# Half 0's new cell ahead of half 1's sum on VectorE, and half 0's cell tanh ahead of half 1's gate tanh on ScalarE, in a four-layer residual stack

## The reference, cut to what matters

```python
def step(carry, xw_t):
    prev_h, prev_c = carry
    A = xw_t + prev_h @ Wh
    i = jax.nn.sigmoid(A[:, 0:Hdim])
    f = jax.nn.sigmoid(A[:, Hdim:2 * Hdim])
    o = jax.nn.sigmoid(A[:, 2 * Hdim:3 * Hdim])
    g = jnp.tanh(A[:, 3 * Hdim:4 * Hdim])
    next_c = f * prev_c + i * g
    next_h = o * jnp.tanh(next_c)
    return ((next_h, next_c), next_h)
```

## Time and profile before

| | |
|---|---|
| median of 3 runs | 3879.23 us (3876.97 to 3882.91) |
| the profiled execution | 3882.09 us |
| its span, first to last instruction | 3880.3 us |
| TensorE matmul / VectorE / ScalarE / GpSimd busy | 3606.7 / 3369.5 / 1632.7 / 784.1 us |
| chain that ended last | VectorE 69%, TensorE 21%, issue 5%, ScalarE 4% |

### The profile page before, as it was taken

One profiled execution on the slowest core, in us unless ns is written; L12 is line 12 of the kernel. 1 busy time (PEld: TensorE's weight loads), 2 busy tenths in 40 slices (PEclk: granted clock), 3 DMA queues, 4 the chain that ended last, 5 costly groups with the idle time before them and its releaser, 6 DMA issues.

```text
span 3880.3 us, 256505 instructions
## 1 busy us (share of the span) xinstructions
PE 3606.7 (93%) x110398; PEld 3050.5 (79%) x110398; DVE 3369.5 (87%) x21169; ACT 1632.7 (42%) x8276; POOL 784.1 (20%) x3623
## 2 busy tenths in 40 slices
PE   7899999999999999999999999999999999999875
PEld 4688888888888888888888888888888888887754
DVE  6598888888898889888888898888888888888876
ACT  4244444444444444444444444444444444444332
POOL 1122222222222222222222222222222222222111
PEclk9999999999999999999999999999999999999999
DMA  7100000000000000000000000000000000000000
GB/s 278 49 7 7 10 10 10 7 7 10 10 10 10 8 7 9 10 10 10 10 7 7 10 10 10 10 7 7 10 10 10 10 9 7 9 7 7 7 6 8
DMA packets 19126, 63.41 MB, mean 16 GB/s; under 512 B 3958, under 2 KB 4526, under 8 KB 14914
## 3 DMA queue, kind: packets, MB, share of 16 engines
q1 hardware_dynamic: 17692, 46.67, 3.8%
q10 hardware_dynamic: 294, 0.33, 0.0%
HBM read 38.48 MB, written 8.39 MB: 12 GB/s over the span
## 4 chain that ended last, share of the span: by engine, by line
DVE 69%; PE 21%; issue 5%; ACT 4%; DMA 1%; POOL 0%; SPq 0%; ACTq 0%; DVEq 0%; POOLq 0%
DVE lstm_sums L743 20%; PE ps_lstm L1045 18%; DVE ps_lstm L748 9%; DVE lstm_ig_fc L754 6%; DVE rnn_sums L851 6%; DVE ps_lstm L759 4%; DVE lstm_h_parts L783 4%; DVE rnn_h_parts L861 3%; DVE lstm_h_scaled L780 3%; DVE rnn_h_parts L866 2%; DVE ps_rnn L759 2%; DVE lstm_h_parts L787 2%; DVE lstm_gates_2c L763 2%; DVE ps_rnn L856 2%; ACT rnn_h L506 2%
## 5 line engine op out<-in xcount | busy, mean ns | idle before, releaser
L1045 PE MATMUL ps_lstm<-lstm_Wh_parts,lstm_h_parts 128*20 128x256 f16 x65472 | 1971.5, 273 | 230.1 <-DVE lstm_h_parts L787 154.9
L1045 PEld LDWEIGHTS ps_lstm<-lstm_Wh_parts,lstm_h_parts 128*20 128x20 f16 x65472 | 1564.5, 91 | 612.2 <-DVE lstm_h_parts L787 486.4
L483 ACT ACTIVATE lstm_gates_2c<-ps_lstm 128x32 f32<-128x32 f32 x2048 | 405.0, 198 | 1416.4 <-DVE ps_lstm L748 1416.4
L743 DVE STREAM_TRANSPOSE lstm_sums<-ps_lstm 128x256 f32<-128x256 f32 x2048 | 912.6, 446 | 84.2 <-PE ps_lstm L1045 44.6
L347 POOL COPY lstm_sums<-lstm_in 128x32 f32<-128x32 f32 x2048 | 427.7, 211 | 1749.7 <-DVE ps_lstm L748 1749.7
L1084 PE MATMUL ps_rnn<-rnn_Wh_parts,rnn_h_parts 128*20 128x128 f16 x32736 | 640.8, 220 | 26.1 <-DVE rnn_h_parts L866 22.1
L1084 PEld LDWEIGHTS ps_rnn<-rnn_Wh_parts,rnn_h_parts 128*20 128x20 f16 x32736 | 546.6, 92 | 67.9 <-DVE rnn_h_parts L866 47.4
L748 DVE TENSOR_REDUCE ps_lstm<-lstm_sums 128x32 f32<-128x96 f32 x2048 | 554.5, 271 | 34.2
L488 ACT ACTIVATE lstm_o_scaled<-lstm_gates_2c 128x8 f32<-128x8 f32 x2048 | 426.9, 208 | 32.3
L783 DVE TENSOR_TENSOR lstm_h_parts<-lstm_o_scaled,lstm_tanh_c 128x8 f16<-128x8 f32 x2048 | 332.4, 162 | 108.4
L506 ACT ACTIVATE rnn_h<-ps_rnn 128x16 f32<-128x16 f32 x1024 | 188.6, 184 | 521.3 <-DVE ps_rnn L856 521.3
(11 more groups left out here) (189 smaller groups left out, 3140.0 us busy)
## 6 DMA issues: line engine op xcount, KB each, us to landing
layer_plus_2I<-in_L_cond_w SPq DMA_DIRECT2D x16, 1024.0 KB, 6.4
out<-out_rows SPq DMA_DIRECT2D x128, 64.0 KB, 1.7
x_rows<-in_x SPq DMA_DIRECT2D x31, 256.0 KB
lstm_Wx<-in_L_cond_Wh SPq DMA_DIRECT2D x1, 4096.0 KB, 17.9
lstm_Wx<-in_L_cond_Wx SPq DMA_DIRECT2D x1, 4096.0 KB, 13.6
layer_plus_2I<-in_L_cond_Wh SPq DMA_DIRECT2D x1, 1024.0 KB, 8.7
rnn_Wx<-in_L_cond_Wx SPq DMA_DIRECT2D x1, 1024.0 KB, 11.0
lstm_in<-in_L_cond_w SPq DMA_DIRECT2D x1, 1024.0 KB, 9.9
```

Source lines behind the costliest of these rows:

```text
L743: return mark(V.transpose(tr[h][s % 2][:, :, 0:QC], psL[h][:, 0:HW].rearrange("p (g c) -> p g c", c=QC)))
L1045: ins = mm(psL[h][QC * j:QC * j + LO + NB, 0:HW], hls[:, k, :], whl[:, k, h, e, j, :], start=(k == 0 and e == 0), stop=(k == KB - 1 and e ...
```

## The change

Two calls change places, each with its neighbour. No instruction is added, removed or altered, and every wait stays with its call. On ScalarE the cell tanh of half 0 now stands in front of the gate tanh of half 1. On VectorE the new cell of half 0 stands in front of half 1's sum.

```diff
@@ -495,8 +495,8 @@
                     if w["lstm"]:
                         gates(0, s)
                         out_gate(0, s)
+                        tanh_cell(0, s)
                         gates(1, s)
-                        tanh_cell(0, s)
                         out_gate(1, s)
                         tanh_cell(1, s)
                     if s == 0 and p["rnn"]:
@@ -884,8 +884,8 @@
                         reduce(0, s, at)
                         at = transpose(1, s)
                         p_at = products(0, s)
+                        new_cell(0, p_at)
                         reduce(1, s, at)
-                        new_cell(0, p_at)
                         if w["rnn"]:
                             r_at = transpose_rnn(s)
                         p_at = products(1, s)
```

## The result

The changed kernel takes 4048.46 us (median of 5 runs, 4046.80 to 4049.59) against 3879.23 before: a ratio of 1.0434, 95% interval 1.0423 to 1.0445, that is 169 us slower. The forecast was 4045 in 4030 to 4066. The profiled execution took 4048.1 with a span of 4046.3, 166.0 more than the span before; the prediction had put it at 4048. Most of the 3.5 us between the forecast and the median are the 2.9 that the prediction took off because the profiled execution before lay above its median; the one after does not.

The account below looks back on a forecast made before the run. The prediction took a 3.58 us step loop through VectorE and TensorE as the bound, VectorE alone in some steps. 1024 × 0.165 = 169, less 2 to 4, gave +166: 4045 us by median, range 4030 to 4066.

Parts of the forecast that it names:

- The new cell waits for products 0: VectorE: half 0's new cell needs its products' result, so it starts 0.035 us after they end and VectorE idles.
- Its slot in front of the sum: VectorE: half 1's sum starts 0.075 us behind the new cell, at 2095.42 instead of 2095.25, 0.165 later.
- Sum 1, gate tanh 1, products 1 have no slack: Half 1's sum, gate tanh and products all come 0.165 us later, moving TensorE's start by the same.
- Nothing is gained by the early tanh: Half 0's h stands behind half 1's products, so its earlier cell tanh gains nothing; bounds 0.01 gained, 0.03 lost.
- Swallowed time: Steps where TensorE is late by itself absorb 0.03 us each, 2 to 4 us in all.
- The ScalarE swap costs nothing: ScalarE: half 0's cell tanh ends at 2095.715, just as half 1's gate tanh is ready, so nothing is lost.
- the sum that waits until the new cell has finished: Rival on VectorE: half 1's sum comes 0.29 us late in place of 0.165, giving 4173 us; 3 in 100.
- Products 1 hang on the gate tanh: Half 1's products follow its gate tanh by 0.03; the rival has the RNN's transpose hold them, 3976 us, 3 in 100.
- The rival in which TensorE's clock falls: Rival: TensorE's clock falls in the last 32 steps, at most 43 us on top, 4088 us; 2 in 100.

Follow-up runs that it names:

- The filler in that wait: Changed kernel with one more VectorE instruction, on constants and waiting for nothing, between half 0's products and its new cell: 4048.20 us.
- fillers: Kernel before with one or two added VectorE instructions, on constants and waiting for nothing, in front of half 1's sum: 3919.38 us with one, 3999.56 with two.
- the runs with the added matmuls: Three more matmuls a step on TensorE in the last chunk: 4046.05 us on the changed kernel, 4049.64 on the kernel with the VectorE swap alone.
- the order that uses the early tanh: Changed kernel with half 0's h and high part in front of half 1's products, and half 1's new cell last: 3975.88 us.

## Why the prediction was right

The mechanism and the number held, step by step.

- *The new cell waits for products 0.* Forecast 0.035 behind their end. In the step shown the cell starts at 2183.25, 0.03 behind 2183.06 + 0.16. The filler in that wait, which cost nothing, shows that VectorE idles there.
- *Its slot in front of the sum.* Forecast 0.075, measured 0.08 to 0.09 (2183.25 to 2183.34); in return the sum lasts 0.26 and not 0.27. The two nearly cancel: sum 1 starts 0.17 later and ends 0.165 later. The prediction had neither of these two small errors in view; that they cancel is luck, worth some 7 us.
- *Sum 1, gate tanh 1, products 1 have no slack.* Shown by fillers: 80 us for 0.077 more.
- *Nothing is gained by the early tanh.* The VectorE swap alone takes the same time as both. Half 0's h stands behind products 1, 0.10 as before.
- *Swallowed time.* Forecast 2 to 4 us. Added up over all steps, TensorE's start behind the low part of half 0 came 2.4 us closer. 1024 × 0.165 is 169, less 2.4 and plus the 1.6 of the clock in the last chunk is 168; the span grew by 166.0. The last 2 us are within what one execution differs from another, so the hit to the microsecond is luck, the one to the few is not.
- *The ScalarE swap costs nothing.* Right in the changed kernel, but only because the later sum hides it: alone it costs 140 us. The prediction found the cell tanh ending just as the gate tanh becomes ready, and did not say that this holds only beside the other edit.

Of the rivals, the sum that waits until the new cell has finished would have given 4173; it starts 0.09 behind the cell's start, while the cell lasts 0.17. The Trainium skill, page "VectorE: DVE Perf Modes", section "The DRAIN you can't avoid", has the next op wait for an empty pipe, and adds that an op that is not held, by a rule that it gives further on, starts earlier. The prediction quoted the first half only. The runs go against it for these instructions and with the second: starts are 0.08 to 0.09 apart at 0.17 each. Products 1 hang on the gate tanh (0.03 behind it) and not on the RNN's transpose. The rival in which TensorE's clock falls came true for 3.4 us of the last chunk, where I had written that the level should stay: I had compared the busy share of ordinary steps and not the steps of the last chunk, whose gaps grew from 1.65 and 1.83 us in the kernel before to 1.82 and 2.03. The price, 1.6 us, is far below the bound of 43. The page "TensorE: Matmul & The Clock Gate" of the Trainium skill, in its section "Why this matters for your kernels", warns of idle gaps between bursts; the runs with the added matmuls agree in direction, though the gaps here are shorter than the one it warns of.

The misses were in the experiments: the spacing behind a 16-element product, in front of an instruction without a wait, is 0.08 where I took 0.09 to 0.11 (41 us for one filler, not 65 to 85), the gate tanh follows a cell tanh after 0.08 where I took 0.09 to 0.17 (140, not 171 or more), and in the order that uses the early tanh VectorE's own queue, which sets the time of many steps, was left out (3976, not 3943).

## What to carry to other kernels

In an in-order queue an instruction moved forward takes its wait with it: ask when its operand is ready and who stands behind it, and not how early its own reader could start. Two halves that share a queue are a balance; before favouring one, look for the instruction of the other half that its reader also stands behind. And price two edits both together and each alone when they delay the same instruction: here 169 and 140 make 169, and either of them undone by itself would have left most of the loss.

## What the runs showed of the hardware that was not expected

- A gate tanh (128x32) starts 0.08 us behind the start of a cell tanh (128x8) that lasts 0.18, and then lasts 0.19 in place of 0.20; the cell tanh behind a gate tanh starts after 0.10.
- Half 1's sum lasts 0.26 instead of 0.27 right behind a small instruction that writes PSUM (a filler or the new cell), with the same shape and data. There it also no longer waits for its transpose; which of the two shortens it no run separates.
- TensorE's clock fell to the 1.2 GHz level in the middle of a chunk that had run at 2.4 GHz, behind idle gaps of 1.8 to 2.0 us a step; before the change, with gaps of 1.65 to 1.83 in the same chunk, it did not, nor with gaps of up to 1.98 behind two fillers. Three matmuls a step in the gaps kept it up in the two kernels with the fall that were given them; each of these is one execution. Whether a given execution falls is not fixed by the gaps alone: the changed kernel's execution had one stretch, that of the VectorE swap alone three, with the same gaps up to the first.
